# TensorE's order in the layer attention: pairs of tiles against four tiles at once

## The reference

```python
def _attn(x, W_qkv, b_qkv, W_ao, b_ao):
    qkv = jnp.einsum('bsd,od->bso', x, W_qkv) + b_qkv      # 16 heads of 8 features
    ...
    scores = jnp.einsum('bhqd,bhkd->bhqk', q, k) * SCALE
    wts = jax.nn.softmax(scores, axis=-1)
    o = jnp.einsum('bhqk,bhkd->bhqd', wts, v)
    o = jnp.moveaxis(o, 1, 2).reshape(b, s, d)
    return jnp.einsum('bsd,od->bso', o, W_ao) + b_ao
for l in range(4):
    x = _ln(x + _mamba(x, ...)); x = _ln(x + _attn(x, ...)); x = x + _mlp(x)
```

## Time and profile before

| | before |
|---|---|
| median of 3 runs | 3382.39 us |
| profiled execution | 3401.33 us |
| its span | 3399.7 us |
| TensorE busy | 3106.2 us (91%) |
| VectorE busy | 1895.0 us (56%) |
| ScalarE busy | 1763.0 us (52%) |
| GpSimd busy | 801.6 us (24%) |
| mean granted TensorE clock | 0.899 |

### The profile page before, as it was taken

How to read it: one execution, slowest core, us unless ns; L and a number is a source line. 1 busy time by engine, 2 the same in 40 slices (tenths; PEclk the granted TensorE clock), 3 DMA queues, 4 the chain that set the end, 5 groups by cost and what they waited for, 6 DMA issues and landing times.

```text
span 3399.7 us, 57274 instructions
## 1 busy us (share of the span) xinstructions
PE 3106.2 (91%) x17396; PEld 1885.0 (55%) x17396; DVE 1895.0 (56%) x3116; ACT 1763.0 (52%) x2669; POOL 801.6 (24%) x864
## 2 busy tenths in 40 slices
PE   7899999799999799999899997999966999799999
PEld 4445546445546455455445445666644777466666
DVE  5557725567636567436557445454436788444444
ACT  6346655356745367555357555444431666544443
POOL 0112200122100122100112113445442000144444
PEclk8869979779999689699579798999987999899999
DMA  2224300234200333100334100000001323000000
GB/s 90 54 73 107 78 6 7 64 86 100 62 5 7 83 93 97 39 12 8 85 81 100 39 11 1 1 0 0 0 0 62 97 92 97 6 4 6 3 6 6
DMA packets 95850, 150.50 MB, mean 44 GB/s; under 512 B 13152, under 2 KB 81248, under 8 KB 89312
## 3 DMA queue, kind: packets, MB, share of 16 engines
q1 hardware_dynamic: 95712, 148.77, 16.6%
HBM read 79.00 MB, written 67.11 MB: 43 GB/s over the span
## 4 chain that ended last, share of the span: by engine, by line
PE 58%; issue 17%; POOL 10%; DVE 6%; DMA 4%; SPq 2%; ACT 2%; POOLq 1%; DVEq 0%; ACTq 0%
PE ps L948 11%; POOL hhlo L2188 9%; PE ps L973 9%; PE ps L754 3%; PE ps L995 2%; DVE hmx L1858 2%; PE ps L717 2%; PE ps L681 2%; PE ps L687 2%; PE ps L793 2%; PE ps L829 1%; PE ps L1163 1%; PE ps L960 1%; PE ps L941 1%; DMA hqk<-hqk_scratch 1%
## 5 line engine op out<-in xcount | busy, mean ns | idle before, releaser
L1858 DVE TENSOR_REDUCE hmx<-ps 128x2 f32<-128x512 f32 x1024 | 689.8, 689 | 361.7 <-PE ps L948 358.1
L1454 ACT ACTIVATE hpt<-ps 128x1024 f32<-128x1024 f32 x512 | 524.4, 1024 | 445.1 <-PE ps L960 445.1
L948 PE MATMUL ps<-hqk 24*128 24x256 f32 x2048 | 530.5, 375 | 73.0 <-DMA hqk<-hmt 26.0
L948 PEld LDWEIGHTS ps<-hqk 24*128 24x128 f32 x2048 | 337.4, 218 | 438.7 <-DVE hmx L1858 252.8
L2188 POOL TENSOR_TENSOR hhlo<-hh,hhh 128x512 fp32r<-128x512 f32 x320 | 412.9, 1290 | 463.9 <-ACT hhh L1533 462.9
L960 PE MATMUL ps<-hqk 26*128 26x256 f32 x2048 | 521.7, 373 | 0.1
L1528 ACT ACTIVATE sil<-ps 128x512 f32<-128x512 f32 x320 | 190.9, 596 | 442.4 <-PE ps L1165 438.4
L973 PE MATMUL ps<-hpt,hvx 128*32 128x256 f32 x4096 | 388.7, 458 | 0.4
L1952 DVE TENSOR_TENSOR su<-ps,sil 128x512 f32<-128x512 f32 x256 | 177.0, 692 | 326.8 <-PE ps L1165 318.6
L960 PEld LDWEIGHTS ps<-hqk 26*128 26x128 f32 x2048 | 326.7, 216 | 54.3 <-issue 43.2
L1533 ACT ACTIVATE hhh<-hh 128x512 fp32r<-128x512 f32 x320 | 199.3, 623 | 40.9 <-DVE hh L1955 26.9
(11 more groups left out here) (247 smaller groups left out, 5627.1 us busy)
## 6 DMA issues: line engine op xcount, KB each, us to landing
hqk_scratch<-hqks SPq DMA_DIRECT2D x256, 192.0 KB, 3.1
hqk<-hqk_scratch SPq DMA_DIRECT2D x256, 192.0 KB
qk_scratch<-qks SPq DMA_DIRECT2D x16, 768.0 KB, 3.3
k<-qk_scratch SPq DMA_DIRECT2D x16, 384.0 KB
qv<-qk_scratch SPq DMA_DIRECT2D x64, 96.0 KB
mw<-mw_in SPq DMA_DIRECT2D x10, 516.5 KB, 3.9
w12raw<-w_in SPq DMA_DIRECT2D x1, 2560.0 KB, 9.6
streams<-x_in SPq DMA_DIRECT2D x8, 256.0 KB, 4.5
```

What stands on the lines that cost most here:

```text
L948: return mm(ps[:, o % 2, qt * SEQ:(qt + 1) * SEQ], hqk[r][32 * g:32 * g + 24, 0, j, qt * P:(qt + 1) * P], hqk[r][32 * g:32 * g + 24, 1, j, ...
L1454: A(hpt[:, j, g:g + 2, :, :], ps[:, 2 + g:4 + g, :], ACT.Exp, scale=QSCALE).then_inc(hd_exp, 1)
L1858: V.tensor_reduce(hmx[:, r, :, 4 * g + j], ps[:, o % 2, :].rearrange("p (t k) -> p t k", t=2), AX.X, ALU.max).then_inc(hd_max, 1)
```

## The change

In `step` of TensorE the order inside a part is written anew; nothing changes on the other engines, and no matmul is added or taken away.

- Before, a part issued for u = 0 and then u = 1: `row` half 0, `score` half 0, `row` half 1, `score` half 1, so two row tiles of the array at a time, each u with its own wait for VectorE (`o + u - 2`: the bank's own last use). Between u = 0 and u = 1 stood a half of `values` in six or seven of the eight parts.
- Now a part waits once, for maximum `o - 1`, which means that both row banks have been read. Then come both heads' `row` and both heads' `score` of half 0, then the same four of half 1.
- `values` is issued whole (both kt, 8 matmuls) behind the eight matmuls of the part: j = 3 of the sequence before in part 1, j = 0 in part 3, j = 1 in part 5, j = 2 in part 6.
- `out` moves from the head of part 7 to its end.

```diff
-                def values(b, j, kt, r):
+                def values(b, j, r):
...
-                    for g in range(GROUPS):
-                        last = mm(ps[32 * g:32 * g + 32, 6, (j // 2) * SEQ:(j // 2 + 1) * SEQ], hvx[r][:, kt, g, j, :],
-                                  hpt[:, j, g, kt, :], start=j % 2 + kt == 0, stop=j % 2 + kt == 2)
-                    if kt == 1:
-                        last.then_inc(hd_pv, 1)
+                    for kt in range(2):
+                        for g in range(GROUPS):
+                            last = mm(ps[32 * g:32 * g + 32, 6, (j // 2) * SEQ:(j // 2 + 1) * SEQ],
+                                      hvx[r][:, kt, g, j, :], hpt[:, j, g, kt, :],
+                                      start=j % 2 + kt == 0, stop=j % 2 + kt == 2)
+                    last.then_inc(hd_pv, 1)
...
                         pe.wait_ge(hd_exp, nth(hd_exp, B, p - 2))
-                        for u in range(2):
+                        if both:
+                            pe.wait_ge(hd_max, nth(hd_max, B + ahead, o - 1))
+                        for t in range(2):
                             if both:
-                                pe.wait_ge(hd_max, nth(hd_max, B + ahead, o + u - 2))
-                                row(o + u, ra, 0)
-                            score(2 * p + u, r, 0)
-                            if both:
-                                row(o + u, ra, 1).then_inc(hd_am, 1)
-                            last = score(2 * p + u, r, 1)
-                            if u == 1:
-                                last.then_inc(hd_sc, 1)
...
+                                for u in range(2):
+                                    last = row(o + u, ra, t)
+                                    if t == 1:
+                                        last.then_inc(hd_am, 1)
+                            score(2 * p, r, t)
+                            last = score(2 * p + 1, r, t)
+                        last.then_inc(hd_sc, 1)
```

More of the change, by code:

```diff
@@ L962, in score @@
                               hqk[r][32 * g:32 * g + 26, 0, j, :], start=True, stop=True)
-                def values(b, j, kt, r):
+                def values(b, j, r):
                     B = l * BATCH + b
-                    if kt == 0:
-                        pe.wait_ge(hd_exp, nth(hd_exp, B, 2 * j + 1))
-                    if j == 0 and kt == 0:
+                    pe.wait_ge(hd_exp, nth(hd_exp, B, 2 * j + 1))
+                    if j == 0:
                         pe.wait_ge(hd_raw, nth(hd_raw, B - 1))
                         pe.wait_ge(hd_v, nth(hd_v, B))
-                    for g in range(GROUPS):
-                        last = mm(ps[32 * g:32 * g + 32, 6, (j // 2) * SEQ:(j // 2 + 1) * SEQ], hvx[r][:, kt, g, j, :],
-                                  hpt[:, j, g, kt, :], start=j % 2 + kt == 0, stop=j % 2 + kt == 2)
-                    if kt == 1:
-                        last.then_inc(hd_pv, 1)
+                    for kt in range(2):
[4 more added lines that the diff above has]
+                    last.then_inc(hd_pv, 1)
                 def maxima(b):
@@ L1006, in step @@
                     for p in range(8):
[L1007 to L1012, removed]
                         if p == 0:
@@ L1049, in step @@
                         if p == 1 and not first:
-                            values(b - 1, 3, 1, (r + 3) % 4)
+                            values(b - 1, 3, (r + 3) % 4)
                         if p == 2 and n3:
@@ L1053, in step @@
                             project_qk(b + 3)
+                        if p == 3:
+                            values(b, 0, r)
                         if p == 4 and not first:
@@ L1061, in step @@
                             sums(b - 1)
-                        if p == 5 and n1:
-                            if first:
-                                pe.wait_ge(hd_q, nth(hd_q, B + 3, 1))
+                        if p == 5:
+                            values(b, 1, r)
+                            if n1:
+                                if first:
+                                    pe.wait_ge(hd_q, nth(hd_q, B + 3, 1))
+                                else:
+                                    pe.wait_ge(hd_ln, nth(hd_ln, B - 1))
+                                maxima(b + 1)
+                        if p == 6:
+                            values(b, 2, r)
+                        if p == 7 and not first:
+                            if n1:
+                                pe.wait_ge(hd_mt, nth(hd_mt, B + 1))
                             else:
                                 pe.wait_ge(hd_ln, nth(hd_ln, B - 1))
-                            maxima(b + 1)
+                            out(b - 1)
                 def last():
-                    values(15, 2, 1, 3)
-                    values(15, 3, 0, 3)
-                    values(15, 3, 1, 3)
+                    values(15, 3, 3)
                 def first_qk():
```

## The result

The changed kernel took 3264.7 us in the median of four runs (3262.08 to 3267.46), the kernel before beside it 3383.89 (3382.23 to 3455.49): a ratio of 0.9649, interval 0.9631 to 0.9668. The profiled execution took 3267.46 us (span 3265.8) against 3401.33. Runs of the kernel before that lie more than 1.5% above the fastest on the same chip count as slow and are left out of comparisons; the others average 3347.9 to 3383.3 us from chip to chip, so that a ratio to it carries about a percent of doubt, and smaller differences are read from the profiles.

What follows compares the result with a forecast made beforehand. It took TensorE to set the pace at both clock levels, all but alone at 1.2 GHz. From the profiled 3401.33 us, -7 - 32 - 6 - 39 = -84 gave 3317, lowered to 3310 us for the median; range 3268 to 3400.

Steps and rivals of the forecast that it cites:

- The loop: Fast steps: TensorE and VectorE take turns, 1.89 us a part, so a step takes 15.6 us against 15.76.
- the 0.2 for the DMA of the maxima: Fast step, part 0: 0.2 us added because part 0 waits for the DMA that brings the maxima.
- longer turns: Rival for fast steps: a loop of 2.05 us, steps of 16.9, about 3365 us; chance 0.30 together with slow ends.
- the sunken clock: Rival: TensorE's idle time lowers its clock, a fast step becomes 21.6 us, up to 3590 in all; chance 0.10.
- Steps 1 and 2: Low-clock time behind step 0: the clock is up after a third of step 1, -32 us.
- Step 0: First step of each layer's attention: the forecast sum held no term for it.
- Middles: Middles of the layers: -7 us from 45 fast steps and -6 us from less time at low clock.
- +10 against it for new falls: Middles: 10 us set against a gain of 16, as part 0 has little work and more idle time.
- Ends: Last steps of the four layers: 45 us in each, together 180 against 219 us, -39 us.
- The 7 us for the median's distance to the profile: Whole kernel: the sum of 3317 us lowered to 3310, since less low clock should bring median and profiled execution closer.
- the same dense work follows itself sooner: Steps at low clock: with small matmuls packed, values and projections follow sooner, so the clock is up a third into step 1.

Runs made afterwards that it cites:

- the pairs: The changed kernel with each part's small matmuls again issued as two pairs, each waiting for its own bank: 3242.82 us, ratio 0.9643 to the kernel before.
- half reads: The changed kernel with VectorE's maxima taken over half of the columns only, leaving out part of the computation: 3267.9 us, ratio 0.9715 to the kernel before.

## Why the prediction was wrong

- **The loop** (1.89 us a part): right to the hundredth. The fast step is 7 x 1.88 + 2.30 = 15.46 us instead of 15.6: `minus_max` costs 0.42 and not 0.3, and the 0.2 for the DMA of the maxima doesn't show in it. The rivals of longer turns and of the sunken clock did not come.
- **Steps 1 and 2** (-32): -34. Right, though for more than packing: 105 us at 1.2 GHz became 38.
- **Step 0** (0, and not even a term): -12. The clock now rises 8.6 us into it, at 188.6 us in layer 0.
- **Middles** (-7 and -6): -29. By the fast step 0.28 x 40 = 11 us; the rest is low clock, 55 us down to 14. I had put +10 against it for new falls, and they did not come.
- **Ends** (-39): -59, the largest miss. The forecast of the new ends, 4 x 45 = 180 us, was right: 178.7. The step that failed is the term for the old ones, 219 us, read from `add_out` to `add_out`. In the old order the last of these belongs to the `out` at the head of part 7 of step 15; behind it come that part, with a half of `values` in it, and three more halves, at 1.2 GHz, until 462.70. From `project_v` to the last `values` the old ends are 237.4 us. Between the prediction's own marks they are 58.2 + 44.8 + 61.5 + 57.5 = 221.9 us, so some 3 us come from layers 2 and 3 taken as layer 0, and 15 from the mark: the change moved `out`, and `add_out` with it.
- The four deviations are -2, -12, -16 and -20 us, -50 together, against -50 between the sum of 3317 and the profiled 3267. The 7 us for the median's distance to the profile were too much: the new kernel's runs lie within 5 us.
- **What the prediction said of the cause** failed as well. It gave the gain to four tiles at once; by the pairs, that is neutral to slightly costly. It costed the move of `out` at nothing, and gave the idle time of TensorE as a reason for the clock to sink. What the runs show as the gain is one dense piece behind both pairs of every part: whole `values` in four parts, a projection or `sums` in each of the others, with `out` closing the hole between parts 7 and 0. Nearest to what ran was its remark that the same dense work follows itself sooner, but it put that down to the packed small matmuls. That the total still came within 2% is in part luck. The Trainium skill, TensorEngine Tiling (Array Packing), section PSUM Bottleneck, says that tiling quickens TensorE but not the reading of PSUM. The half reads agree that the reading is in the loop (1.89 to 1.44 us a part); as throughput alone it was not the limit, with VectorE busy for 115.64 of 154.80 us.

Open: what exactly makes the clock fall or stay low. The rows put the falls behind parts with little or no dense work, and move them when those parts are moved, but tie them to no single quantity. A run that adds a useless dense piece in the hole, and nothing else, would test it; there is none.

## What to carry to other kernels

Order small packed matmuls as neighbours and put one whole dense piece behind them in every turn, so that it runs while the other engine reads both banks. Look for turns without a dense piece: here the clock fell behind them, and moving one piece there was worth some 100 us. Measure a stretch between marks that the change doesn't move, and cost an edit at nothing only after asking what it does to the clock. Let tiles on free row strips join by themselves; a joint wait for both banks cost 0.7 us a step here.

## What the runs showed of the hardware

- The clock went against the busy share: TensorE was busy for 40.00 of 40 us and for 14.98 of 16 us at 1.2 GHz, and for 122.54 of 154.80 us at 2.4.
- With whole `values` and `out` at the head of part 7, the clock fell in 28 of 40 steps, always within 2.0 us after `project_v`, behind 2.3 to 2.5 us without a dense piece. With part 4 emptied instead, it fell behind part 4.
- Row tiles issued as two pairs with separate waits start 0.01 us apart if both are free (299.81, 299.82), as tightly as four issued together.
- A reduction of 128x1024 over two banks took 1.23 us, two of 128x512 1.29, and the large one began 0.64 us after the matmuls instead of 0.54.
- The longer instruction of `minus_max` takes 0.76 us in the changed kernel, where a GpSimd operation starts 0.01 us ahead of it (297.84 and 297.85). In the pairs kernel it starts 0.01 us ahead of that operation and takes 0.19, while the operation is about as long as before. In layer 0 of both kernels, each time that the two overlap, it is the one that starts first that decides:

```profile
296.32 0.19 DVE L1857 SCALAR_TENSOR_TENSOR hhl<-hmx,hhl 128x32 fp32r<-128x32 f32 x1
296.33 0.77 POOL L2138 TENSOR_TENSOR hqks<-hqk,hqks 128x256 fp32r<-128x256 f32 x1
```
